# A decoder layer on one core: the FFN products of the last two tiles on VectorE, and the calls of the attention and FFN stage in another order

## The reference

```python
x = layernorm(x + mamba_and_mixture_of_experts(x))
x = layernorm(x + cross_attention(x, ctx))      # 16 heads of 128, 64 keys for each batch entry
x = layernorm(x + ffn(x))                       # width 704, fp8 rounding of inputs, hidden values and weights
```

## Time and profile before

| What | us |
|---|---|
| Median of 3 runs (lowest, highest) | 696.58 (692.29, 697.43) |
| The profiled execution's own time | 693.12 |
| Its span, first to last instruction | 691.4 |
| TensorE busy in the span | 596.8 (86%) |
| VectorE busy | 465.3 (67%) |
| ScalarE busy | 394.6 (57%) |
| GpSimd busy | 304.3 (44%) |
| Mean granted TensorE clock | 0.950 of full |

### The profile page before, as it was taken

The page is one execution under the profiler, slowest core; times in us unless marked ns, Lnnn a source line. Parts: engine busy times, 40 slices in busy tenths (PEclk is TensorE's granted clock), DMA queues, the critical chain, the costliest instruction groups (busy, mean ns, idle before and its releaser), DMA issues.

```text
span 691.4 us, 10825 instructions
## 1 busy us (share of the span) xinstructions
PE 596.8 (86%) x3611; PEld 461.3 (67%) x3611; DVE 465.3 (67%) x768; ACT 394.6 (57%) x864; POOL 304.3 (44%) x235
## 2 busy tenths in 40 slices
PE   4989987878878799899999898999979999998642
PEld 2546576767767677698789787889834555555521
DVE  5979799999899966533434432533444788899775
ACT  4668699999899927332222321311626475778441
POOL 4041079999799986124232324244111323233221
PEclk9997799999999999999999999999989999999865
DMA  7001081212111116423423440411610000000001
GB/s 262 1 0 54 25 343 49 61 49 59 46 49 59 31 46 229 154 75 146 160 57 139 150 150 30 159 32 30 212 46 0 1 0 1 0 1 0 1 0 62
DMA packets 17119, 51.43 MB, mean 74 GB/s; under 512 B 2706, under 2 KB 8467, under 8 KB 15411
## 3 DMA queue, kind: packets, MB, share of 16 engines
q1 hardware_dynamic: 14098, 41.43, 17.0%
q0 software_dynamic: 2688, 7.34, 3.6%
q10 hardware_dynamic: 288, 2.10, 0.8%
HBM read 45.95 MB, written 4.92 MB: 74 GB/s over the span
## 4 chain that ended last, share of the span: by engine, by line
PE 41%; ACT 22%; DVE 15%; DMA 9%; issue 7%; POOL 5%; POOLq 1%; SPq 0%; DVEq 0%; ACTq 0%
ACT arena L588 10%; PE ps L1944 9%; ACT arena L599 8%; PE ps L1952 7%; PE ps L2013 5%; DMA moe_out<-arena,result_now 5%; PE ps L2002 3%; PE ps L2034 2%; DVE arena L988 2%; PE ps L1801 2%; DMA arena<-hn_rows,row_now 2%; POOL arena L480 1%; POOL arena L394 1%; DMA arena<-hn_rows,row_of 1%; PE ps L2025 1%
## 5 line engine op out<-in xcount | busy, mean ns | idle before, releaser
L394 POOL TENSOR_TENSOR arena<-arena 128x1024 f32<-128x1024 f32 x64 | 150.9, 2373 | 45.6 <-DVE arena L1185 40.9
L1185 DVE TENSOR_TENSOR_SCAN arena<-arena,ps 128x1024 f32<-128x1024 f32 x64 | 146.1, 2285 | 11.5 <-POOL arena L394 8.3
L1944 PEld LDWEIGHTS ps<-arena 128*128 128x128 f32 x924 | 106.1, 192 | 5.0 <-issue 4.3
L1944 PE MATMUL ps<-arena 128*128 128x128 f32 x924 | 107.2, 276 | 0.8 <-issue 0.3
L1758 PE MATMUL ps<-ident,arena 128*128 128x128 f32 x512 | 68.6, 277 | 31.0 <-ACT arena L599 23.2
L759 ACT ACTIVATE arena<-ps 128x256 f32<-128x256 f32 x63 | 24.2, 384 | 112.4 <-PE ps L1944 112.2
L588 ACT ACTIVATE arena<-arena,a_neg 128x510 f32<-128x510 f32 x128 | 84.6, 709 | 3.7 <-DVE arena L1185 3.7
L1758 PEld LDWEIGHTS ps<-ident,arena 128*128 128x128 f32 x512 | 55.0, 140 | 44.1 <-ACT arena L599 41.7
L599 ACT ACTIVATE arena<-arena,b_tok 128x512 f32<-128x512 f32 x128 | 84.4, 709 | 0.0
L1776 PE MATMUL ps<-ident,arena 128*128 128x128 f32 x512 | 66.5, 273 | 0.5 <-POOL arena L394 0.5
L1952 PE MATMUL ps<-arena 128*128 128x256 f32 x252 | 61.2, 395 | 0.0
(11 more groups left out here) (289 smaller groups left out, 1028.9 us busy)
## 6 DMA issues: line engine op xcount, KB each, us to landing
arena<-in_w_moe SPq DMA_DIRECT2D x8, 2176.0 KB, 9.2
arena<-c_dram SPq DMA_DIRECT2D x32, 256.0 KB, 3.2
arena<-in_w_o ACTq DMA_DIRECT2D x1, 2048.0 KB, 8.8
arena<-in_w_qT SPq DMA_DIRECT2D x1, 2048.0 KB, 9.9
arena<-moe_out SPq DMA_DIRECT2D x4, 512.0 KB, 5.7
arena<-in_w_q SPq DMA_DIRECT2D x1, 2048.0 KB, 12.9
x<-in_x SPq DMA_DIRECT2D x2, 512.0 KB, 4.4
arena<-in_w_in SPq DMA_DIRECT2D x2, 512.0 KB, 5.7
```

The lines of the kernel that those rows point to most:

```text
L394: pool.tensor_tensor(in_chunks(hC[:, unit % 2, :]), in_chunks(h[:, unit % 2, :]), c_bc[:, m % C_BUFS, :].unsqueeze(1).to_broadcast([P, 2, ...
L1185: nc.vector.tensor_tensor_scan(h[:, k, :], dA[:, k, :], ps[:, 2 * k:2 * k + 2, :].rearrange("p a b -> p (a b)"), 0.0, ALU.mult, ALU.add).t ...
L1944: ins = nc.tensor.matmul(ps[:, bank, c * P:(c + 1) * P], w13[:, k, chunk * P:(chunk + 1) * P], xT[:, k, :], start=(k == 0), stop=(k == KD ...
```

## The change

`product(t)` becomes a function of VectorE as well, with the same waits; GpSimd's calls for tiles 6 and 7 go, and VectorE makes them instead. Tiles 0 to 5 keep their product on GpSimd. Beyond that the lists of ScalarE, VectorE and TensorE for the stage are written in another order; no call is added or dropped. The diff, cut: of the first tiles only the beginning is shown, of the last three tiles everything.

```diff
@@ gpsimd
             product(5)
             tile_rstd(6)
             tile_rstd(7)
-            product(6)
-            product(7)
@@ scalar
             take_transposed_probs(0, 0)
             take_transposed_probs(0, 1)
-            mean_squares(2, 0, 1)
             exponential(1)
+            mean_squares(2, 0, 1, 2, 3)
             scale_tokens(0)
-            mean_squares(2, 2, 3)
...
             take_transposed_probs(5, 0)
+            take_transposed_probs(5, 1)
             take_tokens(4)
-            take_transposed_probs(5, 1)
+            mean_squares(7, 0)
+            silu_of(4)
             exponential(6)
-            silu_of(4)
-            mean_squares(7, 0)
-            take_hidden(3)
             mean_squares(7, 1)
             scale_hidden(4)
+            mean_squares(7, 2, 3)
+            take_hidden(3)
             scale_tokens(5)
-            mean_squares(7, 2, 3)
             take_tokens(5)
             take_transposed_probs(6, 0)
             take_transposed_probs(6, 1)
+            exponential(7)
             silu_of(5)
             take_hidden(4)
-            exponential(7)
             scale_hidden(5)
+            scale_tokens(6)
+            take_hidden(5)
             take_transposed_probs(7, 0)
+            take_tokens(6)
             take_transposed_probs(7, 1)
-            take_hidden(5)
-            scale_tokens(6)
-            take_tokens(6)
             silu_of(6)
+            scale_hidden(6)
             scale_tokens(7)
-            scale_hidden(6)
             take_tokens(7)
             silu_of(7)
             take_hidden(6)
@@ vector
+            def product(t):
+                dve.wait_ge(s["ff_gate"], t + 1)
+                dve.wait_ge(s["ff_read"], t + 1)
+                if t:
+                    dve.wait_ge(s["t_in_ready"], t)
+                nc.vector.tensor_tensor(prod, gate_s[:, t % 2, :], up_s[:, t % 2, :], ALU.mult).then_inc(s["prod_done"], 1)
...
+            add_epsilon(0)
             take_scores(0)
-            add_epsilon(0)
             scale_scores(0)
...
             take_scores(7)
-            scale_scores(6)
+            add_epsilon(6)
+            add_result(2)
             take_gate(4)
             take_up(4)
-            softmax(6)
+            scale_scores(6)
             add_attention(5)
             scale_of_hidden(4)
             scale_of_tokens(5)
+            softmax(6)
+            add_epsilon(7)
             round_hidden(4)
             round_tokens(5)
-            add_epsilon(7)
             add_result(3)
+            scale_scores(7)
             take_gate(5)
             take_up(5)
-            scale_scores(7)
+            softmax(7)
+            add_attention(6)
             scale_of_hidden(5)
-            add_attention(6)
-            softmax(7)
+            scale_of_tokens(6)
             round_hidden(5)
+            round_tokens(6)
             add_result(4)
-            scale_of_tokens(6)
-            round_tokens(6)
-            add_attention(7)
             take_gate(6)
             take_up(6)
+            product(6)
+            scale_of_hidden(6)
+            add_attention(7)
             scale_of_tokens(7)
-            scale_of_hidden(6)
+            add_result(5)
             round_tokens(7)
             round_hidden(6)
             take_gate(7)
             take_up(7)
             variances("bn5", "eps5", OUT_PARTS[0])
-            add_result(5)
+            product(7)
             scale_of_hidden(7)
             dve.wait_ge(s["rstd_out"], 1)
             normalise("out_done", OUT_PARTS[0])
@@ tensor
...
-            queries_of(6, 1, 2)
+            scores_of(7)
+            transpose_hidden(2)
+            queries_of(6, 2, 3)
+            transpose_probs(5)
             down(2)
-            queries_of(6, 3)
-            scores_of(7)
-            transpose_probs(5)
             transpose_tokens(4)
             queries_of(7, 0)
             gate_of_tokens(4)
             up_of_tokens(4)
-            transpose_hidden(3)
             values_of(5)
             queries_of(7, 1)
+            transpose_hidden(3)
+            queries_of(7, 2, 3)
             down(3)
-            queries_of(7, 2, 3)
             transpose_probs(6)
             transpose_tokens(5)
             gate_of_tokens(5)
             up_of_tokens(5)
             transpose_hidden(4)
             values_of(6)
             down(4)
+            transpose_hidden(5)
             transpose_probs(7)
-            transpose_hidden(5)
-            values_of(7)
             transpose_tokens(6)
             gate_of_tokens(6)
             up_of_tokens(6)
+            values_of(7)
             down(5)
             transpose_tokens(7)
```

More of the change, by code:

```diff
@@ L840, in _ @@
             take_transposed_probs(0, 1)
-            mean_squares(2, 0, 1)
             exponential(1)
+            mean_squares(2, 0, 1, 2, 3)
             scale_tokens(0)
-            mean_squares(2, 2, 3)
             take_transposed_probs(1, 0)
+            take_tokens(0)
             take_transposed_probs(1, 1)
-            take_tokens(0)
+            mean_squares(3, 0)
             exponential(2)
             silu_of(0)
-            mean_squares(3, 0)
+            mean_squares(3, 1, 2)
             scale_hidden(0)
+            mean_squares(3, 3)
             scale_tokens(1)
-            mean_squares(3, 1, 2)
+            mean_squares(4, 0)
             take_tokens(1)
-            mean_squares(3, 3)
-            take_hidden(0)
             take_transposed_probs(2, 0)
             take_transposed_probs(2, 1)
-            mean_squares(4, 0)
+            mean_squares(4, 1)
             silu_of(1)
@@ L862, in _ @@
             scale_hidden(1)
-            mean_squares(4, 1)
+            take_hidden(0)
             scale_tokens(2)
@@ L866, in _ @@
             take_tokens(2)
+            mean_squares(5, 0)
             take_transposed_probs(3, 0)
             take_transposed_probs(3, 1)
[L869 removed]
             exponential(4)
             silu_of(2)
+            take_hidden(1)
             mean_squares(5, 1, 2)
             scale_hidden(2)
[L874 removed]
+            mean_squares(5, 3)
             scale_tokens(3)
[L876 to L877 removed]
             take_transposed_probs(4, 0)
             take_transposed_probs(4, 1)
[L880 to L881 removed]
+            take_tokens(3)
             exponential(5)
             silu_of(3)
[L884 removed]
+            mean_squares(6, 0, 1)
             scale_hidden(3)
[L886 removed]
+            take_hidden(2)
             scale_tokens(4)
+            mean_squares(6, 2, 3)
             take_transposed_probs(5, 0)
+            take_transposed_probs(5, 1)
             take_tokens(4)
[L890 removed]
+            mean_squares(7, 0)
+            silu_of(4)
             exponential(6)
[L892 to L894 removed]
             mean_squares(7, 1)
             scale_hidden(4)
+            mean_squares(7, 2, 3)
+            take_hidden(3)
             scale_tokens(5)
[L898 removed]
             take_tokens(5)
@@ L1475, in _ @@
             scale_of_tokens(1)
+            round_hidden(0)
+            add_epsilon(3)
             round_tokens(1)
-            round_hidden(0)
             take_scores(3)
-            add_epsilon(3)
+            scale_scores(3)
             take_gate(1)
             take_up(1)
-            scale_scores(3)
             add_attention(2)
@@ L1485, in _ @@
             scale_of_tokens(2)
+            take_scores(4)
+            round_tokens(2)
             round_hidden(1)
-            take_scores(4)
+            add_epsilon(4)
             softmax(3)
-            add_epsilon(4)
-            round_tokens(2)
-            add_result(0)
             take_scores(5)
             scale_scores(4)
+            add_result(0)
             take_gate(2)
@@ L1499, in _ @@
             scale_of_tokens(3)
+            add_result(1)
             round_hidden(2)
+            add_epsilon(5)
             round_tokens(3)
-            add_epsilon(5)
             take_scores(6)
-            add_result(1)
             scale_scores(5)
@@ L1511, in _ @@
             scale_of_tokens(4)
-            add_result(2)
             round_hidden(3)
-            add_epsilon(6)
             round_tokens(4)
             take_scores(7)
-            scale_scores(6)
+            add_epsilon(6)
+            add_result(2)
             take_gate(4)
             take_up(4)
-            softmax(6)
+            scale_scores(6)
             add_attention(5)
@@ L2097, in _ @@
             values_of(1)
-            queries_of(3, 1, 2)
+            queries_of(3, 2, 3)
             scores_of(3)
+            queries_of(4, 0)
             transpose_tokens(1)
-            queries_of(3, 3)
-            transpose_hidden(0)
             transpose_probs(2)
-            queries_of(4, 0)
+            queries_of(4, 1)
             gate_of_tokens(1)
@@ L2108, in _ @@
             scores_of(4)
-            queries_of(4, 1, 2, 3)
+            transpose_hidden(0)
+            queries_of(4, 2, 3)
+            scores_of(5)
+            queries_of(5, 0)
```

(17 more changed lines are left out.)

10 lines of the change are left out of this document (1 added, 9 removed).

## The result

The changed kernel takes 690.62 us (median of 14 runs, 686.96 to 691.59). 14 runs of the kernel before on the same chip gave 694.49 (691.82 to 697.43). The ratio is 0.9942, with a 95% interval of 0.9925 to 0.996: 0.6% faster, which is clear of zero and under the 1% that the chances were about.

A forecast was written before the change was run, and what follows sets the result against it. TensorE bounds the first part, VectorE the middle, a dependent chain the end. Tail gains 1.3 + 1.6 = 2.9 us, the middle's 0.9 loss being paid back: 696.58 - 2.9 = 693.7 us, range 687.5 to 699.0.

The forecast's parts named there:

- the chances: Whole kernel: faster by over 1% 0.15, slower by over 1% 0.09, within 1% 0.76.
- The bound of each stretch: TensorE bounds 511.3 to 635.9 us, VectorE and its waits 635.9 to 651.0, one dependent chain of tile 7 the rest.
- My call-by-call count: First part: each call starts after its engine's previous call and its waits; tile 7's queries end at 634.2, before 635.8.
- VectorE as second bound: First part: VectorE works 15.8 us of about 17 a tile, so only about 1.2 us a tile to spare.
- The middle: 634 to 651 us: softmax(7) ready 4 us earlier, but round_hidden(5) ends at 651.1, so 0.9 us are lost.
- the price of the new order: Middle: silu_of(5) behind exponential(7) needs a 1.28 us load, ends at 643.8 instead of 641.15; product(5) starts 2.5 us later.
- The tail: After 651 us: take_up(7) ends 1.3 us earlier, then 1.6 gained to scale_of_hidden(7), 2.9 us in sum.
- The rule on VectorE and GpSimd: Middle: two-input VectorE and SBUF-reading GpSimd instructions exclude one another, so product(5) keeps 2.54 us; alone, 0.8 earlier.
- the first: Rival, after 651 us: a shorter TensorE gap keeps the clock at 2.4 GHz; 8.6 us with the 2.9, 688.0; chance 0.13.
- The second: Rival, first part: VectorE holds TensorE up at transpose_probs, costing 3.0 plus 1.8 us, 698.5; chance 0.15.
- the third: Rival, tail: its two gains vanish through a later product(5) and values_of(7) at the low clock, 696.6; chance 0.22.

The follow-up runs named there:

- e7: New kernel with the products of tiles 0 to 5 on VectorE too, each ahead of its scale_of_hidden: stage 173.73 us, ratio to the kernel before 1.0035.
- e5: New kernel with one swap on ScalarE, silu_of(5) ahead of exponential(7): stage 170.48 us, ratio to the kernel before 0.9975.
- e6: New kernel with values_of(7) ahead of tile 6's transpose, gate and up, ScalarE's and VectorE's calls in step: stage 171.0 us, ratio to before 0.9974.
- e4: Kernel before's lists up to up_of_tokens(4), then the new lists with products of tiles 6 and 7 on VectorE: stage 172.18 us, ratio to before 0.9966.
- e10: New kernel with unused matmuls on TensorE in three gaps, behind down(4), down(5) and down(6): stage 165.46 us, ratio to the kernel before 0.9916.
- e2: New kernel's order with product(6) and product(7) back on GpSimd: stage 170.39 us, ratio to the kernel before 0.9972.
- e11: New kernel unchanged, run again as a control: stage 169.46 us, ratio to the new kernel's first measurement 0.9985.

## Why the prediction was right

The forecast was 2.9 us faster; the ratio of the first measurement gives 0.0058 x 694.5 = 4.0, and the stage gives 3.4. The time itself, 690.62 for 693.7, is 3.1 off, and 2.1 of that lies in the starting point: the median of 3 runs of the kernel before was 696.58, that of 14 is 694.49. Point by point, in the forecast's time (the new trace less 1.39 us):

| Event, its end | Before | Forecast | After |
|---|---|---|---|
| V5 (values_of(5)) | 630.05 | 628.7 | 628.3 |
| Tile 7's last queries | 635.9 | 634.2 | 633.8 |
| round_hidden(4) | 636.7 | 637.3 | 636.9 |
| silu(5) | 641.15 | 643.8 | 643.4 |
| round_hidden(5) | 650.8 | 651.1 | 650.9 |
| V7 | 658.8 | 660.6 | 659.9 |
| take_up(7) | 672.1 | 670.8 | 670.1 |
| scale_of_hidden(7) | 676.4 | 673.5 | 672.7 |
| Span | 691.4 | 688.5 | 687.7 |

**The bound of each stretch: right for two, wrong for the first.** I wrote that the same matmuls in another order "can give at most the 0.64 us of idle time back". They gave 1.4. V5 starts 107.87 us after the first queries before and 106.12 after; 0.34 of that is transpose_hidden(3), which moved behind it, and nothing else crossed V5. The clock isn't the cause. TensorE in nine slices of 12 us from the first queries, sum of the slices (every slice 1.00), first the kernel before, then the new one:

```profile
sum 108.00, PE 107.39 PEld 59.78 DVE 84.05 ACT 71.33 POOL 32.81; mean PE 11.93 PEld 6.64 DVE 9.34 ACT 7.92 POOL 3.65
```

```profile
sum 108.00, PE 108.00 PEld 61.46 DVE 85.77 ACT 71.68 POOL 31.47; mean PE 12.00 PEld 6.83 DVE 9.53 ACT 7.96 POOL 3.50
```

0.61 us of idle time that could be seen went to zero. The other 0.8 couldn't be seen: a call's end is modelled and laps over the next (V5 from 626.02 for 3.62 ends at 629.64, but the next call starts at 629.48), so a wait of up to 0.16 us at a change of call counts as busy. Start against start was the measure to use. My call-by-call count did this and gave 634.2, and I explained its difference to 635.8 by rounding. The count was better than the cap that I had put on it.

**VectorE as second bound: right.** TensorE never waited visibly before 626. e7 shows the margin: with 0.9 us a tile more TensorE stood, and V5 came 1.6 us later.

**The middle: right in its times, wrong in what I called its price.** silu(5) ended 2.3 us later than before (forecast 2.7), product(5) took 2.51 (2.54), and round_hidden(5) stood where it had. But I called the late silu "the price of the new order". VectorE waits only 0.37 us for product(5), and is busy for 14.08 of 15.10 us: it does softmax(7) and scale_of_tokens(6) in that time. e5 ends silu(5) 1.6 us earlier, at the price of a second load ahead of exponential(7), and is 1.3 us slower. It was an exchange, and a good one.

**The tail: right, two terms a little too large.** The two transposes, gate and up of tile 6 and V7 took 8.95 us; I had 9.4, since gate and up took 2.27 for both and I had 1.33 each. V7's fall from 5.46 to 3.62 came as said, and e6 shows what the place of the gates is worth, 1.8 us. The new product at 0.89 was forecast at 0.9, L1346 at its own 0.17, and take_up(7) to the end of scale_of_hidden(7) took 2.6 us, forecast 2.7, before 4.3.

**The rule on VectorE and GpSimd.** The Trainium skill, SBUF — State Buffer, section Who interferes with whom, was to hold here, and by it I kept product(5) at 2.54. It took 2.51, so the trace agrees. e4 shows the other turn of the same pair: GpSimd first, at 1.68, and VectorE stretched to 2.37.

**The rivals.** The clock stayed low (0.72, 0.67), so the first didn't come. I had priced it at 8.6 - 2.9 = 5.7 us beyond the forecast; e10, which nearly forces it, gives 3.7: 1.9 where I had 2.5 (to the end of V7), 1.1 where I had 1.3 (to take_up(7)), and 0.7 where I had 1.9 (the rest, where the clock is still 0.63 at the end). That VectorE is the reason is likely, not shown: in the three stretches at full clock it is busy for 5.78 of 7.03, 7.94 of 9.13 and 6.96 of 7.20 us. The rival's condition, a shorter gap, is not what keeps the clock up or down by itself, as the gaps of e5 and e7 show. The second had no waits to show, and of the third nothing vanished.

The profiled execution's own time, 690.82 for 690.2, looks closer than the steps were. The forecast was 0.4 us too late up to silu(5) and 0.8 at the end, and the execution happened to begin its stage 1.4 us later; that the two nearly cancel is luck.

## What to carry to other kernels

Where in-order engines hand work to one another, count an order call by call with start-to-start times, and judge it whole: here the first half brought TensorE 1.4 us forward, and with the old lists behind it the kernel was 0.6 us slower. Read a half's trace before its time: e4 lost 1.3 us to a clock that fell behind the same waits as in eight other traces. A product moved off GpSimd gains twice, by its own time and by the VectorE instructions that it no longer stretches, but only as long as VectorE has time to spare (two tiles gained about 1 us; all eight cost 4.5 us more than the two). And where one dependent chain ends a kernel, look at the granted clock beside TensorE's gaps: matmuls whose result nobody reads, cut to the length of the gap, were worth more than the whole change.

## What the runs showed of the hardware

- Unused matmuls in three gaps kept the granted clock at 1.00 instead of about 0.7 and took 3.7 us off the stage; the same filler 3.5 us too long lost 1.2 us. The filler was on TensorE alone, and nothing else was slower by more than 0.3 us.
- A VectorE multiply and a GpSimd product that meet run one behind the other, whichever is first: 1.68 with 2.37 (e4), and 2.51 with 1.23 (new kernel, L1387 from 644.63). For this pair I had counted only on GpSimd being late.
- The time before the first queries, identical code, moved between 518.51 and 528.18 us over 14 traced executions. Gains under 1% are read from a stage, not from the total. What moves it was not tried.
- The granted clock isn't set by the waits just ahead alone: behind the same two waits (1.94 and 0.49 us) it fell in e4 and stayed at 1.00 in eight traces. And it was up again sooner behind a gap of 5.72 us (gate and up 1.41, e7) than behind 5.20 (2.53, e2 and e11).
- A change of activation table took 1.28 us with nothing behind it: the next ACTIVATE starts 0.01 us after the load's end.
